# Router in column strips, and a last sequence whose tokens fill an expert's slots from the top, in a windowed-attention and MoE kernel

## What is computed

```python
x = x + attn(layernorm(x), Wq, Wk, Wv, Wo)      # 16 heads of width 8, causal window of 64
x = x + ffn(layernorm(x), w_router, w1, w2, bias)

# ffn: E = 8 experts, top 2, capacity = 2 * 8192 / 8 = 2048 slots for each expert
scores = softmax(xf @ w_router)                 # xf: 8192 x 128, w_router: 128 x 8
expert_weights, top_experts = top_k(scores, 2)
order = argsort(flat_e, stable=True)            # earlier tokens get the earlier slots
valid = offsets < capacity                      # those beyond 2048 are dropped
h = gelu(einsum('ech,ehf->ecf', xb, w1))        # 128 -> 512
y = einsum('ecf,efh->ech', h, w2)               # 512 -> 128
out = zeros.at[src].add(flat_w[order] * yv) + bias
```

## Time and profile before

| | |
|---|---|
| median of 3 runs | 835.31 us (834.75 to 837.74) |
| the profiled execution | 842.32 us |
| its span (first to last instruction) | 840.6 us |
| PE busy | 737.9 us (88%) |
| DVE busy | 499.3 us (59%) |
| ACT busy | 449.9 us (54%) |
| POOL busy | 356.4 us (42%) |
| mean granted TensorE clock | 0.953 of 2.4 GHz |

### The profile page before, as it was taken

One profiled execution on the slowest core, in us unless ns is written; L12 is line 12 of the kernel. 1 busy time (PEld: TensorE's weight loads), 2 busy tenths in 40 slices (PEclk: granted clock), 3 DMA queues, 4 the chain that ended last, 5 costly groups with the idle time before them and its releaser, 6 DMA issues. The chain is left out here.

```text
span 840.6 us, 18825 instructions
## 1 busy us (share of the span) xinstructions
PE 737.9 (88%) x7293; PEld 519.0 (62%) x7295; DVE 499.3 (59%) x1620; ACT 449.9 (54%) x923; POOL 356.4 (42%) x318
## 2 busy tenths in 40 slices
PE   6999999999999999999999996249998888989982
PEld 3555565565566566566566564216987778978872
DVE  7888888988888888878878878401213112212210
ACT  5576686686686586586686663103443333433430
POOL 3000000033233233233233254663877877877876
PEclk9999999999999999999999997559999999999996
DMA  4952000000010000000000011113455555555533
...
DMA packets 49122, 50.27 MB, mean 60 GB/s; under 512 B 5905, under 2 KB 39336, under 8 KB 48016
## 3 DMA queue, kind: packets, MB, share of 16 engines
...
...
## 5 line engine op out<-in xcount | busy, mean ns | idle before, releaser
L434 POOL DMA_INDIRECT out<-y_sb,xg x128 | 198.6, 1552 | 68.3 <-issue 51.7
L355 POOL DMA_INDIRECT slots_dram<-rows_sb,slot_id x128 | 126.1, 985 | 218.0 <-PE sT_ps L1118 177.8
L677 DVE TRANSPOSE_TENSOR_REDUCE kmax<-sT_ps 128x32 f32<-128x1024 f32 x128 | 159.6, 1246 | 13.8 <-PE sT_ps L1101 13.6
L510 ACT ACTIVATE probsT<-sT_ps 128x1024 f32<-128x1024 f32 x128 | 132.4, 1035 | 60.9 <-PE sT_ps L1118 59.5
L609 ACT ACTIVATE hT<-sT_ps 128x512 f32<-128x512 f32 x128 | 76.6, 598 | 150.0 <-PE sT_ps L1329 138.8
L1101 PE MATMUL sT_ps<-qbd,kT 64*128 64x256 f32 x1024 | 132.5, 378 | 0.0
L1038 DVE TENSOR_TENSOR y_sb<-o_ps,xg 128x256 f32<-128x256 f32 x32 | 13.6, 425 | 183.5 <-DMA out<-y_sb,xg 100.3
L1329 PE MATMUL sT_ps<-xT_hl,w_hl 128*128 128x512 f32 x384 | 102.5, 418 | 22.5 <-DVE xT_hl L1028 16.1
L372 POOL TENSOR_TENSOR xbias<-x_sb,bias_sb 128x256 f32<-128x256 f32 x32 | 23.4, 731 | 192.9 <-PE sT_ps L1118 192.9
L1101 PEld LDWEIGHTS sT_ps<-qbd,kT 64*128 64x128 f32 x1024 | 98.0, 190 | 9.6
L1329 PEld LDWEIGHTS sT_ps<-xT_hl,w_hl 128*128 128x128 f32 x384 | 73.6, 198 | 40.7 <-DVE xT_hl L1028 16.7
...
## 6 DMA issues: line engine op xcount, KB each, us to landing
...
slots_dram<-rows_sb,slot_id POOLq DMA_INDIRECT x128
out<-y_sb,xg POOLq DMA_INDIRECT x128
...
```

Of the source, the lines that this page charges most:

```text
L355: pool.indirect_dma_start(out=slots_dram, out_offset=bass.IndirectOffsetOnAxis(ap=slot_id[:, g % 2, k, j:j + 1].bitcast(U32), axis=0), in_ ...
L434: pool.indirect_dma_start(out=out, out_offset=bass.IndirectOffsetOnAxis(ap=xg[:, r, 4 * c + k, ROW - 1:ROW].bitcast(U32), axis=0), in_=y_s ...
L510: nc.scalar.activation(probsT[:, gp].rearrange("p b k h q -> p (b k h q)"), sT_ps[:, gp].rearrange("p b c -> p (b c)"), ACT.Exp).then_inc( ...
L677: nc.vector.tensor_reduce(kmax[:, u % 2, :], sT_ps[:, u % 2].rearrange("p b (c q) -> p (b c) q", q=32), AX.X, ALU.max, apply_transpose=Tru ...
```

## The change

1. **Router.** `router` computes the logits of all eight token tiles at the end of tile 5's slot, with the operands swapped: the stationary operand is a new `wr_cols` (the 8 router columns in a strip of 32, at column 0 for k = 0 and at column 8 for k = 1), the moving one is `xn2T`, 128 tokens at a time, and the four results go to the four strips of 32 output partitions. The two halves accumulate in one place. ACT copies the result to `lgT_sb` at the end of its slot of tile 5, PE transposes it at tile 6 (`router_T`), and DVE reads the logits from there. POOL prepares `wr_cols` at the start. The last sequence keeps its own router.
2. **Slots of the last sequence.** In `positions` for sequence 7 the slot is the expert's last slot less the position in the sequence (`elast - pos`), not the running count plus position. Two steps (the new count, the addition of `eslot`) go, one (`r_end`) comes. The test for the capacity is as it was.
3. **Loads.** A chunk is now 512 consecutive slots. SP loads chunks 0 and 1 of expert 0 when the sends of the first seven sequences have landed, and chunks 2 and 3 when those of the last have (`s_scat_last`).
4. **Start of the expert phase.** PE does not wait for `s_near` (which is gone) and issues 30 matmuls of zeros in place of 62. In the first expert the transposes of chunk 2 come after the results of chunk 1, with 20 matmuls of zeros between. DVE does `slots_lo` of chunk 1 before the gating of chunk 0.

```diff
@@ SP
-            slots_e = slots_dram.rearrange("(e p j) w -> p e (j w)", e=E, p=P)
-            def load_slots(e, r):
-                for c in range(CHUNKS):
+            slots_e = slots_dram.rearrange("(e c p j) w -> p e c (j w)", e=E, c=CHUNKS, p=P)
+            def load_slots(e, r, chunks=range(CHUNKS)):
+                for c in chunks:
                     sp.dma_start(xg[:, r:r + 1, 4 * c:4 * c + 4, :].rearrange("p o j w -> p o (j w)"),
-                                 slots_e[:, bass.ds(e, 1), 4 * c * ROW:4 * (c + 1) * ROW]).then_inc(ld_g[r][c], 16)
+                                 slots_e[:, bass.ds(e, 1), c, :]).then_inc(ld_g[r][c], 16)
...
-            sp.wait_ge(s_scat, 16 * TOPK * NTILE)
-            load_slots(0, 0)
+            sp.wait_ge(s_scat, 16 * TOPK * TILES * (BATCH - 1))
+            load_slots(0, 0, range(0, CHUNKS // 2))
+            sp.wait_ge(s_scat_last, 16 * TOPK * TILES)
+            load_slots(0, 0, range(CHUNKS // 2, CHUNKS))
             load_slots(1, 1)
@@ POOL
+                pool.iota(elast[:, :], pattern=[[CAP, E]], base=CAP - 1, channel_multiplier=0,
+                          allow_small_or_imprecise_dtypes=True).then_inc(c_pool, 1)
...
-                    in_offset=None, bounds_check=E * CAP - 1, oob_is_err=False).then_inc(s_scat, 16)
+                    in_offset=None, bounds_check=E * CAP - 1,
+                    oob_is_err=False).then_inc(s_scat_last if g == BATCH - 1 else s_scat, 16)
...
-                        if g == BATCH - 1 and (j, k) == (7, 1):
-                            pool.sem_inc(s_near, 1)
...
+            pool.memset(wr_cols[:, :, :], 0.0).then_inc(c_wr, 1)
             pool.wait_ge(ld_w, 16 * 18)
+            pool.wait_ge(c_wr, 1)
+            for k in range(2):
+                pool.tensor_copy(wr_cols[:, k, k * E:(k + 1) * E], wr_sb[:, :]).then_inc(c_wr, 1)
@@ ACT
+            def logits_T(b):
+                act.wait_ge(s_lgT, b)
+                nc.scalar.copy(lgT_sb[:, :], tail_ps[:, LOGITS:LOGITS + P]).then_inc(s_lgT_sb, 1)
...
                 if not (first and t == 0):
                     context_T(g - 1)
+                if t == 5 and not first:
+                    logits_T(b)
@@ DVE, positions(): part 0, and part 2 (part 3 is left out for the last sequence)
-                    chain.wait()
-                    chain.mark(nc.vector.tensor_tensor(out=r_cnt[:, :], in0=pos[:, TILES, :], in1=r_cnt[:, :],
-                                                       op=ALU.add))
+                    if g == BATCH - 1:
+                        chain.mark(nc.vector.tensor_tensor(out=r_end[:, :, :], in0=elast[:, :].unsqueeze(1).to_broadcast([P, TILES, E]),
+                                                           in1=pos[:, 0:TILES, :], op=ALU.subtract))
+                    else:
...
-                    chain.mark(nc.vector.tensor_tensor(out=r_pos[:, :, :], in0=r_pos[:, :, :], in1=r_t[:, :, :], op=ALU.add))
+                    chain.mark(nc.vector.tensor_tensor(out=r_pos[:, :, :], in0=(r_end if g == BATCH - 1 else r_pos)[:, :, :],
+                                                       in1=r_t[:, :, :], op=ALU.add))
@@ DVE, experts()
+                    if first and c == 0:
+                        slots_lo(q + 1, c + 1)
                     gated(ee, q, c, 0, first)
-                    if not (last and c == 2 * CHUNKS - 1):
+                    if not (first and c < 2 or last and c == 2 * CHUNKS - 1):
                         slots_lo(q + 1, c + 1)
                     gated(ee, q, c, 1, first)
+                    if first and c == 1:
+                        slots_lo(q + 1, c + 1)
@@ PE
-            def router(b, tiles):
-                pe.wait_ge(s_xn2T_sb, 2 * (b - 1) + 1 + max(tiles) // 4)
-                for i in tiles:
-                    last = mm(tail_ps[:, LOGITS + i * E:LOGITS + (i + 1) * E], xn2T[:, i // 4, (i % 4) * P:(i % 4 + 1) * P],
-                              wr_sb[:, :], start=True, stop=True)
-                return last
+            def router(b):
+                pe.wait_ge(s_xn2T_sb, 2 * b)
+                if b == 1:
+                    pe.wait_ge(c_wr, 3)
+                for k in range(2):
+                    for c in range(4):
+                        last = mm(tail_ps[STRIP * c:STRIP * (c + 1), LOGITS:LOGITS + P], wr_cols[:, k, :],
+                                  xn2T[:, k, c * P:(c + 1) * P], start=(k == 0), stop=(k == 1))
+                last.then_inc(s_lgT, 1)
+
+            def router_T(b):
+                pe.wait_ge(s_lgT_sb, b)
+                nc.tensor.transpose(tail_ps[:, LOGITS:LOGITS + P], lgT_sb[:, :], ident[:, :]).then_inc(s_lg, 1)
...
+                    if first and c == CHUNKS // 2 - 1:
+                        results(q, c)
+                        fill_zeros(20)
+                        slots_T(ee, c + 1)
+                        continue
...
-            pe.wait_ge(s_near, 1)
-            fill_zeros(62)
+            fill_zeros(30)
             slots_T(0, 0)
```

29 lines of the change are left out of this document (23 added, 6 removed).

## The result

The changed kernel took 810.25 us (median of 4 runs, 809.18 to 811.28), the kernel before beside it 836.38 (834.75 to 837.74): a ratio of 0.9682, interval 0.9662 to 0.9703. It is faster by 26.1 us where 19.1 were forecast, and just outside the range on its lower side. Measured again on another chip the same kernel gave 830.82 beside 844.24, 13.4 us less, and in a third measurement 811.80 beside 837.51, 25.7 less. So three questions follow: what in the sum was too small, what is different between chips, and what of it can be had everywhere.

The account below looks back on a forecast made before the run. POOL's additions were taken as the bound from the first addition on, PE at the router. From the profiled 842.32, less 6.3 (router), 0.26 (slots) and 12.6 (start), 823.2; 19.1 less than the median 835.31 gives 816.2 us, range 811 to 826.

Parts of the forecast that it names:

- 0.9 x 7 = 6.3 us: Router at tiles 5 and 6: the new products and transposition save 0.9 us in each of seven sequences, 6.3 in all.
- one 128 x 128 transposition ... 0.24 us: Router at tile 6: PE's one new transposition was taken to cost 0.24 us, read from a row of the profile before.
- The tie with ACT's exponentials: Router: exponentials would end at 504.20, PE's next fill needs them at 504.31; 0.1 us a sequence was taken off.
- it may go or come twice: I leave it: Last sequence: POOL's 3.18 us gap between first and second send, counted as nothing, with 3.2 us both ways in the range.
- the 4.6 us that it would have left: Router: if changes of the array's division cost extra, the saving would be up to 1.7 us less, 4.6 instead of 6.3.
- This is paid in full, because the sends are what the first addition now waits for: Slots of the last sequence: one dependent DVE step less brings the first send, and so the end, 0.26 us sooner.
- The start of the experts: From last send to POOL's first addition: early loads and PE start let additions follow 0.30 us behind; 12.6 us without the slots' step.
- Chunk 2 came with 3.2 us to spare where I had 0.6 to 2.2: First expert, ninth addition: chunk 2 ready with 0.6 us to spare, 2.2 if PE's clock holds.
- rival C: First expert: chunk 2 comes late and cold, PE at the lower clock, POOL idle 3.1 us; 819.3 us, chance 0.10.
- rival D: Start of the experts: no overlap as written, first y ready only after the sends, 3.6 us lost; 819.8 us, chance 0.07.
- two gaps such as the 3.18 of POOL: Start of the experts: named, with a wait of the first loads, as what could make PE's start over 9.4 us late.

Follow-up runs that it names:

- the first profile of after: The changed kernel as it is, in its first profiled execution, on a chip with 836.38 us for the kernel before: 809.18 us profiled, median 810.25.
- after_again: The changed kernel, unchanged, measured and profiled again on a second chip, beside 844.24 us for the kernel before: 830.82 us, ratio 0.9837.
- no_zeros: The changed kernel without both fillings, the 30 and the 20 matmuls of zeros on PE: 828.44 us, ratio 0.9807 to the kernel before.
- all but the router: The changed kernel with the old router put back, all other parts of the change kept: 840.30 us, ratio 0.9941 to the kernel before.

## Why the prediction was wrong

The mechanism was right on the chip of the measurement and the sum too small, by 7.0 us (26.1 against 19.1). The steps that failed are two terms of the sum.

The first is the router's, "0.9 x 7 = 6.3 us", built from "one 128 x 128 transposition ... 0.24 us" and the 0.1 taken off for ACT: it brought 1.14 in a sequence and 8.0 in all. The transposition took 0.16. The row that I took has products in 64 rows behind it and this one has full ones, which may be the difference; that was not tested. The tie with ACT's exponentials cost nothing.

The second is a term that I put at nothing: "it may go or come twice: I leave it". The gap between the first two sends of the last sequence fell from 3.18 to 1.22, 2.0 us. On stalling chips it is 3.2 to 3.4 in the profiles without the last sequence's new slots and 2.13 or 2.14 in those with them (1.82 in the one with the bias moved), so 1.1 comes with these parts of the change. The other 0.9 comes where POOL doesn't wait for the slots, and what the kernel before has there on a quiet chip is not known.

Together that is 3.7 of the 7.0. For the rest there is an estimate from the milestones. The profiles differ by 33.1 us. Take off what the profile of before has as one of a stalling chip, 3.3 us in the attention phase and 4.6 at the sends, and 25 us are left: 8.0 for the router, 12.6 for the start, 2.0 for the gap, 2.2 for additions that happened to run 250.4 us in place of 252.6, and little over. So the last 3.3 of the 7.0 are mostly scatter, by this estimate. It hangs on the kernel before not having these waits on a quiet chip; its medians there, 836.4 and 837.5 against 844.2 to 846.2, are 7 to 10 us lower and agree, but there is no profile of it from such a chip.

The changes of the array's division in the router: the trace has 0.57 and 0.16 for the two new steps with the changes inside them, so the rule of the Trainium skill ("TensorEngine Tiling (Array Packing)", "Key Properties"), by which each change drains the engine, takes nothing visible here; the 4.6 us that it would have left are refuted by 8.0.

The slots of the last sequence: "This is paid in full, because the sends are what the first addition now waits for" does not hold for one DVE step less, 0.26. In the first profile of after the slots were ready 3.4 us before POOL came to them, so an earlier slot brings nothing there; POOL's own 32 sends, one behind another, are the chain. Only where ACT stalls does POOL wait for them (4.97 in after_again). The start of the experts: 12.6 forecast without that step, 12.6 in the first pair of profiles, each step within 1.3 us of its row. Chunk 2 came with 3.2 us to spare where I had 0.6 to 2.2, since the clock held (rival C didn't come on this chip).

In after_again, on a stalling chip, rival D ("the first y is ready only after the sends") came true, and half of C, for a reason that neither named. The first y is done at 562.80, the last send at 562.72. Chunk 2 came late, its addition by 6.12 us, but not cold: its first layer took 3.02. PE, ACT and DVE stall beside the sends, y of chunk 1 and with it chunk 2 come late, and of the 12.6 us only 2.4 remain. I had the stall before my eyes, 3.6 us at ACT's copy and POOL's 4.62 for the slots, left both out of the sum, and took "two gaps such as the 3.18 of POOL" for a mishap with a chance of 0.07. Overlapping work with the sends put more of it where they stall it.

The range failed at its lower end by 0.8 us. With the router at 8.0 and the gap at 2.0 less the sum gives 812.5, inside it; what lies below is the part that only the estimate above accounts for.

Open: by what the sends hold up the others. PE's row of 12 products broken in pieces says that it isn't only signals between engines; whether its supply of instructions is held up the traces don't settle. In after_again one transfer of instructions lies at 566.6, 1.5 us before ACT goes on, and others so in no_zeros (0.8) and all but the router (1.4). But none lies at the end of the stall at 528.9, and the undisturbed profile of after has one at 556, also just ahead of work of ACT, with no stall. The Trainium skill ("Runtime: NRT & Kernel Launch", "Instruction fetch mechanics") says that each engine fetches its program in blocks by a DMA queue of its own, mostly hidden; if that is what the sends hold up, it was not hidden here, and no run here shows it. Why the last stall outlives the sends by 5.4 us and why chips differ are open too, and whether a mean of 1.48 us per send or the free window of 2.1 us is what helps: the uniform spacing of that mean ran only where nothing stalls.
